# A shifted-window attention kernel whose first score pass is split into four tiles of 64 rows by 64 columns

## The reference, cut to what matters

```
f = roll(ln(x), (-3, -3));  win = window_partition(f)        # windows of 49 tokens
q, k, v = split(win @ w_qkv + b_qkv)                          # 12 heads of 8 channels
attn = einsum('bhid,bhjd->bhij', q, k) * 8 ** -0.5 + mask     # mask: 0 or -100
attn = softmax(attn);  out = einsum('bhij,bhjd->bihd', attn, v) @ w_proj + b_proj
f = x + roll(window_reverse(out), (3, 3))
y = f + gelu(ln(f) @ w_fc1 + b_fc1) @ w_fc2 + b_fc2
```

## Time and profile before

| what | value |
|---|---|
| median of 3 runs | 2865.55 us (2864.36 to 2867.81) |
| span of the profiled execution, first to last instruction | 2865.7 us |
| TensorE matmuls busy | 2765.1 us (96%) |
| TensorE weight loads busy | 2312.9 us (81%) |
| VectorE / ScalarE / GpSimd busy | 2349.2 / 2136.4 / 1810.7 us |
| mean granted TensorE clock | 0.991 |
| first score pass, L493 | 6144 matmuls, 404.5 us busy |
| DMA engines' share | 46.8% |

### The profile page before, as it was taken

How to read it: one execution, slowest core, us unless ns; L and a number is a source line. 1 busy time by engine, 2 the same in 40 slices (tenths; PEclk the granted TensorE clock), 3 DMA queues, 4 the chain that set the end, 5 groups by cost and what they waited for, 6 DMA issues and landing times.

```text
span 2865.7 us, 137800 instructions
## 1 busy us (share of the span) xinstructions
PE 2765.1 (96%) x55491; PEld 2312.9 (81%) x55491; DVE 2349.2 (82%) x6634; ACT 2136.4 (75%) x3464; POOL 1810.7 (63%) x2344
## 2 busy tenths in 40 slices
PE   4899999999999999999999999999999999999997
PEld 2788888888888888888888888888888888888885
DVE  7788888888888888888888888888888888888885
ACT  2677777777777777777777777777777777777774
POOL 3566666656666666666665665666666666666565
PEclk7999999999999999999999999999999999999998
DMA  2544545444554544454455455454455445454441
GB/s 72 135 125 129 132 124 132 128 130 127 131 133 125 132 131 126 129 132 124 127 132 131 125 133 133 125 132 131 126 132 132 124 129 129 129 132 128 131 117 35
DMA packets 414850, 358.86 MB, mean 125 GB/s; under 512 B 63646, under 2 KB 414176, under 8 KB 414204
## 3 DMA queue, kind: packets, MB, share of 16 engines
q1 hardware_dynamic: 414220, 350.04, 46.8%
HBM read 193.29 MB, written 154.14 MB: 121 GB/s over the span
## 4 chain that ended last, share of the span: by engine, by line
PE 91%; ACT 4%; issue 2%; DVE 2%; POOL 1%; SPq 0%; DMA 0%; POOLq 0%; DVEq 0%
PE psum L529 19%; PE psum L511 11%; PE psum L652 9%; PE psum L437 9%; PE psum L493 8%; PE psum L569 7%; PE psum L554 6%; PE psum L617 6%; PE psum L447 6%; ACT probs L713 4%; PE psum L607 3%; PE psum L455 3%; PE psum L472 2%; PE psum L596 1%; DVE nmax L849 0%
## 5 line engine op out<-in xcount | busy, mean ns | idle before, releaser
L713 ACT ACTIVATE probs<-psum 113x784 f32<-113x784 f32 x768 | 633.2, 824 | 358.9 <-PE psum L511 341.4
L849 DVE TENSOR_REDUCE nmax<-psum 113x16 f32<-113x784 f32 x768 | 745.1, 970 | 97.1 <-PE psum L493 97.0
L529 PE MATMUL psum<-vbd,probs 128*49 128x18 f32 x24576 | 642.4, 197 | 7.6 <-issue 7.0
L398 POOL TENSOR_SCALAR ve<-mv 112x7 f32<-112x7 f32 (+1 forms) x264 | 65.9, 250 | 915.0 <-PE psum L569 672.8
L529 PEld LDWEIGHTS psum<-vbd,probs 128*49 128x49 f32 x24576 | 632.2, 126 | 10.7 <-issue 10.5
L511 PE MATMUL psum<-qbd,kst 128*49 128x196 f16 x6144 | 404.7, 250 | 34.4 <-DVE xfl L884 5.7
L493 PE MATMUL psum<-kbd,qst 128*49 128x196 f16 x6144 | 404.5, 250 | 5.3 <-DVE nmax L849 3.4
L405 POOL TENSOR_TENSOR rs<-ve,half 112x7 f32<-112x7 f32 (+1 forms) x264 | 394.7, 1495 | 0.0
L410 POOL TENSOR_TENSOR xn<-xn,rs 112x672 f32<-112x672 f32 (+1 forms) x264 | 342.6, 1298 | 73.9 <-POOL rs L405 73.9
L884 DVE TENSOR_TENSOR xfl<-psum,xfh 96x784 f16<-96x784 f32 (+1 forms) x264 | 252.9, 958 | 160.7 <-ACT xfh L725 159.6
L873 DVE BATCH_NORM_STATS2 st<-tok 112x6 f32<-112x96 f32 x1824 | 318.1, 246 | 59.0 <-ACT tok L720 45.0
(11 more groups left out here) (96 smaller groups left out, 6129.4 us busy)
## 6 DMA issues: line engine op xcount, KB each, us to landing
stack_pages<-nat SPq DMA_DIRECT2D x256, 294.0 KB, 3.0
kst<-stack_pages SPq DMA_DIRECT2D x256, 220.5 KB
qbd<-stack_pages SPq DMA_DIRECT2D x1024, 55.1 KB
stack_pages<-nat SPq DMA_DIRECT2D x256, 147.0 KB, 2.0
xr<-in_x_dram SPq DMA_DIRECT2D x224, 147.0 KB, 2.7
out_dram<-yr SPq DMA_DIRECT2D x224, 147.0 KB, 2.3
qst<-stack_pages SPq DMA_DIRECT2D x256, 73.5 KB
kbd<-stack_pages SPq DMA_DIRECT2D x1024, 18.4 KB
```

The lines of the kernel that those rows point to most:

```text
L529: last = nc.tensor.matmul(dst[:, :, h, :], probs[:, b.c % 2, h // 4, p, h % 4 * L:(h % 4 + 1) * L], vbd[:, b.c % 4, p * NH + h, :, :], sta ...
L713: nc.scalar.activation(probs[0:PR, b.c % 2, u, :, :].rearrange("j (g q) k -> j g (q k)", g=2), wide_bank()[0:PR, LEFT:LEFT + 8 * SPAN].rea ...
L849: nc.vector.tensor_reduce(dst, psum[0:PR, A:A + 2, 0:2 * CH].rearrange("i g (q h j) -> i g q h j", q=2, j=L), axis=AX.X, op=ALU.max, negat ...
```

## The change

The 392 tokens of a band are cut into two halves s of 196 (PART). The first half keeps its queries and keys in rows 0 to 27 of `qst` and `kbd`, the second gets rows 64 to 91, and both tensors are only 196 tokens long. The 8 matmuls of a group take 64 rows each and run over q (which pair in the half), s (the half: rows 0 or 64, bank A or A + 1) and w (the window: columns 0 or 64). What they compute and where they write it stays. `key_blocks` issues 10 DMAs for a band in place of 5, each with half the tokens (runs of 392 bytes in place of 784), and the mask rows come with 10 in place of 5; the waits count accordingly. The order of the stages on every engine stays.

```
-        kbd = sb("kbd", [FULL, 2, NH, TOK], F16)
-        qst = sb("qst", [FULL, 3, QUADS, TOK], F16)
+        kbd = sb("kbd", [FULL, 2, NH, PART], F16)
+        qst = sb("qst", [FULL, 3, QUADS, PART], F16)
...
-        STACK_IN, KEY_IN = 5 * 16, 5 * 16
+        STACK_IN, KEY_IN = 5 * 16, 10 * 16
...
-                for n in range(2):
-                    sp.dma_start(kbd[QUAD:QUAD + 4, n, :, :], rows_d[2, 0:4]).then_inc(key_masks, 16)
-                for n in range(3):
-                    sp.dma_start(qst[QUAD:QUAD + 4, n, :, :], rows_d[n // 2, 0:4, 0:QUADS, :]).then_inc(key_masks, 16)
+                for s in range(2):
+                    rows, toks = slice(W1 * s + QUAD, W1 * s + QUAD + 4), slice(s * PART, (s + 1) * PART)
+                    for n in range(2):
+                        sp.dma_start(kbd[rows, n, :, :], rows_d[2, 0:4, :, toks]).then_inc(key_masks, 16)
+                    for n in range(3):
+                        sp.dma_start(qst[rows, n, :, :], rows_d[n // 2, 0:4, 0:QUADS, toks]).then_inc(key_masks, 16)
...
-                sp.dma_start(qst[0:QUAD, masked_slot(b), :, :], q_stack[b.c % 4].rearrange("(c a) m t -> m a c t", c=QUADS)[0]).then_inc(key_in[n], 16)
-                for h in range(4):
-                    sp.dma_start(kbd[HD * h:HD * (h + 1), n, h:NH:4, :],
-                                 k_stack[b.c % 4].rearrange("(c h d) m t -> h m d c t", c=QUADS, h=4)[h, 2]).then_inc(key_in[n], 16)
+                for s in range(2):
+                    toks = slice(s * PART, (s + 1) * PART)
+                    sp.dma_start(qst[W1 * s:W1 * s + QUAD, masked_slot(b), :, :], q_stack[b.c % 4].rearrange("(c a) m t -> m a c t", c=QUADS)[0, :, :, toks]).then_inc(key_in[n], 16)
+                    for h in range(4):
+                        sp.dma_start(kbd[W1 * s + HD * h:W1 * s + HD * (h + 1), n, h:NH:4, :],
+                                     k_stack[b.c % 4].rearrange("(c h d) m t -> h m d c t", c=QUADS, h=4)[h, 2, :, :, toks]).then_inc(key_in[n], 16)
...
-                        pe.wait_ge(key_masks, 5 * 16)
+                        pe.wait_ge(key_masks, 10 * 16)
...
-                for p in range(PAIRS):
-                    for w in range(2):
-                        toks = slice((2 * p + w) * L, (2 * p + w + 1) * L)
-                        last = nc.tensor.matmul(psum[W1 * w:W1 * w + L, A + p // 2, p % 2 * CH:(p % 2 + 1) * CH],
-                                                qst[:, masked_slot(b), u, toks], kbd[:, b.c % 2, 4 * u:4 * u + 4, toks], start=True, stop=True)
+                for q in range(2):
+                    for s in range(2):
+                        rows = slice(W1 * s, W1 * s + QUAD + 4)
+                        for w in range(2):
+                            toks = slice((2 * q + w) * L, (2 * q + w + 1) * L)
+                            last = nc.tensor.matmul(psum[W1 * w:W1 * w + L, A + s, q * CH:(q + 1) * CH],
+                                                    qst[rows, masked_slot(b), u, toks], kbd[rows, b.c % 2, 4 * u:4 * u + 4, toks], start=True, stop=True)
```

## The result

The changed kernel took 2897.74 us (2895.4 to 2904.52, 4 runs) beside 2866.68 us of the kernel before: a ratio of 1.0110, interval 1.0097 to 1.0123, some 31 us slower. The forecast was no change, and the time lies 6 us above the range. The profiled execution has a span of 2895.0 us, 29.3 over the one before.

A forecast was written before the change was run, and what follows sets the result against it. The prediction took TensorE's matmul stream to bound the kernel. It summed +5.1 us for pairs of steps, 0 for DMAs, -2.75 and about -2 for the fill: +0.3 us, 2866.0 us, range 2812 to 2892.

The forecast's parts named there:

- What bounds the kernel: Whole kernel: TensorE's matmuls, busy 96% of the span, so a microsecond taken from its stream counts unless another engine's wait follows.
- the gap at a row border: TensorE, where 64-row score matmuls meet 128-row neighbours: each change of division costs a gap of 0.095 us.
- rivals 1 and 3: Row tiles change at little cost, 2788 us, some 2826 at half gap (0.28); four tiles don't run together, 2954 us (0.10).
- Rival 2: Score groups: loads of the lower rows go one behind the other, 0.02 to 0.04 us a group, 2876 to 2886 us (0.16).
- Odd step, scores 0 and scores 1: First two score groups of an odd step: each costs 0.07 us more, as both neighbours had the same division before.
- Even step, scores 0: First score group of an even step: 0.455 us becomes 0.41, as the gap ahead exists already; saves 0.045 us.
- Even step, scores 2: Third score group of an even step: the gap behind it exists already and `on` is ready; saves 0.055 us.
- odd step (expand): Third score group of an odd step: would save 0.055 us, but expand's second half waits for the third maxima; gain 0.
- even step's scores 1: Second score group of an even step: shifted 1 waits for exponentials, leaving 0.24 us of slack; effect 0.
- DMAs: cost 0: SyncE's queue: 5 more issues for each band, 1.7 us, fit into its wait for ScalarE; nothing comes late.
- rival 4: SyncE's queue or the small packets bind, up to 1.7 us a step where keys come late; 2909 us at a tenth (0.04).
- The fill: Start of the kernel: halved zeroing of `kbd` and `qst` saves 2.75 us, shorter score groups about 2 us.

The follow-up runs named there:

- Experiment 3: The kernel before with its 8 score matmuls taking rows 0 to 35 alone (one tile row of 64): 2958.1 us, ratio 1.0319.
- Experiment 4: Even bands take the change's layout, matmuls and 10 DMAs, odd bands stay as in the kernel before: 2857.97 us, ratio 0.9971.
- experiment 2: The kernel before with its 128-row matmuls, but keys and queries read by 10 DMAs of half the tokens in place of 5: 2877.61 us, ratio 1.0047.
- experiment 8: The changed kernel unaltered, run again on another chip: 2897.3 us, ratio 1.0105 to the kernel before.
- experiment 9: The changed kernel with the loops over q and s exchanged, on the same chip as the unaltered changed kernel's rerun: 2896.61 us, ratio 1.0102.
- experiment 7: The changed kernel with the loops over q and s exchanged, first run: 2886.91 us, ratio 1.0079 to the kernel before.
- experiments 1: The kernel before with the 64-row matmuls alone, keeping 392-token tensors and 5 DMAs for each band: 2878.22 us, ratio 1.0041.

## Why the prediction was wrong, point by point

The forecast summed +5.1 us for the pairs of steps, -4.75 for the fill and 0 for the DMAs. In the profiled executions the pairs' median made +19.9, the fill about 0, and pauses, lower clock and late keys, for which the sum had no term, another +9.5. The first is explained by the experiments; the last only in part.

- **What bounds the kernel; four tiles side by side; the gap at a row border.** Right. 0.12 us from first to last start where 0.11 was forecast, gaps of 0.09 to 0.10 at all borders, and rivals 1 and 3 are refuted: no border came cheap and no tile waited. Rival 2 (loads of the lower rows in turn) fell with them: 0.003 us apart.
- **Odd step, scores 0 and scores 1: +0.07 each.** Mis-sized: +0.109 and +0.089. The terms of the group's own sum were short. The stage behind it was given 0.03 for its loads; `weighted`, with float32 weights, takes 0.043 (first to last start 1.082 us, 1.039 in the kernel before where its column tiles are not staggered). The group itself, 0.105 in the sum from first to last start, takes 0.119. And behind `values` the two column tiles ran staggered by half a turn, so that scores 0 began 0.02 us after the last matmul of `values` rather than a whole turn of 0.04; the gap ends that too, another 0.02. Experiment 3 shows the same 1.21 in the chain.
- **Even step, scores 0: -0.045.** -0.029, by the same two terms. Experiment 4 has it alone: -0.033 for a pair.
- **Even step, scores 2: -0.055.** The step of the steady sum that failed in kind, in the path and not in a size. The prediction looked at `on`, which was ready, and not at the exponentials that `back` waits for. Nothing came. It had found the same cover in the odd step (expand), rightly, and in the even step's scores 1.
- Together the pair of steps was forecast at +0.04 and came to +0.166, 20 us in place of 5. In the sum of four small terms of both signs the four errors of 0.016 to 0.055 had the same sign. Five of the nine borders lie on the path, and not six.
- **DMAs: cost 0, rival 4 unlikely.** Wrong. In the undisturbed pair they cost nothing (experiment 2: +0.007 us), and no load of `shifted` waits for `stacks`. But alone they cost the kernel before 11 us. The step that failed is "Nothing ahead is late: keys are read one step before use": in experiment 2 the queue lags in stretches, is on the chain, and keys come up to 1.65 us late, which is rival 4's mechanism at a small part of its price; in the changed kernel it shows in the fill and hardly after. The prediction read the queue in one even step and took its slack of 2.5 us a step as cover for 1.7 us of issues; it left out that the DMAs land later (0.5 us a step). And it had no term for pauses of TensorE at its own instructions and the clock behind them.
- **The fill: -4.75 us.** The shorter zeroing brought the 2.7 us forecast for it. By 68 us TensorE was 6.3 us ahead (in part by full clock in stretches between 42 and 65 us, where the kernel before had the lower one), and late keys and a lower clock took all of it back: 0.
- Rival 2 gave 2876 to 2886 us, nearer to what was measured than the forecast, but not for its reason: its sign, starts spread over 0.13 us and more, did not come (0.119). Rival 1's price at half of the gap is 2830 us by its own working (0.0475 x 6 x 127 = 36), not 2826; nothing rests on it.
- Of the signs named to look for ahead, the starts, the 0.18 us, the untouched shifted 1 and the memsets came. The waits with release "issue" rose by about six a pair of steps, not nine (scores 485 for 125 and `weighted` 385 for 20 from 140 to 2820 us; `shifted` unchanged), and SyncE's queue did not keep its slack.

**What stays open.** Parts don't add up neatly: tiles alone +12, DMAs alone +11, together +31 us. The steady parts nearly do (+0.147 and +0.007, together +0.166). The excess doesn't: in the profiled executions it was 12.2 us before, 4.1 with the tiles alone, 2.3 in experiment 3, 35.0 in experiment 2, 17.6 and 21.7 in the changed kernel. That DMA traffic holds back a fetch is argued, not shown: in the 4 us ahead of the packets that end before a pause the DMA engines are busier than ahead of all 16 KB packets in the changed kernel (0.67 against 0.57) and in experiment 2 (0.68 against 0.57), but not in the kernel before (0.42 against 0.47), which pauses as well. What sets the length of a single pause was not separated. Nor was why a pause is followed by the lower clock in some kernels. From 140 to 2800 us the clock drops three times in the changed kernel, once in experiment 8 and three times in experiment 9, never in experiment 7 and in none of the kernels that keep 128 rows in some bands, nor in experiments 1 and 3; in experiment 2 pauses up to 1.55 us pass without a drop.

## What to carry to other kernels

A group of matmuls that is cut into another division of the array than its neighbours must save more than two gaps of 0.095 us and the loads behind them: here a group of 0.34 us cannot, unless one of its borders is there anyway and nothing else ends the next wait. So place a new division where the engine changes already, and check for each place what ends the next wait, since a saving under an exponential or a maximum is worth nothing. And before a DMA is split, ask of the whole run, not of one step, how much slack the issuing queue has: here five more issues and later landings used up 2.1 of 2.5 us a step, and then keys came late.

## What the runs showed of the hardware that was not expected

- TensorE does not begin matmuls strictly in program order, as read from experiment 7: with both pairs of one tile row ahead of those of the other, four matmuls began within 0.017 us and the last 0.126 us after the first, where strict order would take 0.17; the whole group took 0.007 us more than in the mixed order.
- A group with only one tile row in use pays the same gaps as one with two (0.174 and 0.176 us from the last score matmul to the first of `weighted`).
- TensorE pauses up to 1.55 us in the midst of a stage, 1.2 to 1.6 us after a 16 KB packet of the instruction queue has landed, and at once or soon after the clock may stand at 1.2 GHz for 3.4 to 6.8 us (3.8 us lost for a pause of 1.37).
